# A fused attention and routed-layer kernel: the reads of block numbers gathered at first-layer tiles 2 to 5, one remainder placed inside a routing step, one quarter-sum moved into the next step

## The reference, cut to what matters

```
def _mlp(x, W1, b1, W2, b2):
    return gelu(x @ W1 + b1) @ W2 + b2           # exact gelu, 256 -> 256 -> 256

xn = layernorm(x)
q, k, v = _mlp(xn, ...q), _mlp(xn, ...k), _mlp(xn, ...v)
scores  = (q k^T) / sqrt(256 * 512) * tril       # linear attention, causal, no softmax
x1      = x + layernorm(scores @ v) * ln_w + ln_b
idx     = argmax over 8 tiles of position_table . sign(tile_sigs)     # by position only
out     = x1 + layernorm(x1) @ W[idx].T + b[idx]                      # one of 8 weights per row
```

## Time and profile before

| | us |
|---|---|
| median of 3 runs (lowest, highest) | 304.71 (304.62, 305.18) |
| the profiled execution: its own time | 304.78 |
| its span, first to last instruction | 303.0 |
| PE busy | 281.8 (93%) |
| VectorE busy | 237.2 (78%) |
| ScalarE busy | 191.6 (63%) |
| GpSimd busy | 168.1 (55%) |
| mean granted TensorE clock | 0.992 |

### The profile page before, as it was taken

How to read it: one execution, slowest core, us unless ns; L and a number is a source line. 1 busy time by engine, 2 the same in 40 slices (tenths; PEclk the granted TensorE clock), 3 DMA queues, 4 the chain that set the end, 5 groups by cost and what they waited for, 6 DMA issues and landing times.

```text
span 303.0 us, 5527 instructions
## 1 busy us (share of the span) xinstructions
PE 281.8 (93%) x1818; PEld 252.7 (83%) x1818; DVE 237.2 (78%) x549; ACT 191.6 (63%) x389; POOL 168.1 (55%) x230
## 2 busy tenths in 40 slices
PE   6869999999899999999999999999999898999970
PEld 6757988898789889888978898989898898999850
DVE  4587879889988978986898689678856879867660
ACT  2278568767666776678667866876877445787000
POOL 3902452172459184937554663648374476777771
PEclk9999999999999999999999999999999999999996
DMA  7816991002111211021121100017021460693220
GB/s 199 285 53 175 358 294 35 0 2 69 35 39 37 80 63 38 6 100 39 38 88 52 68 7 0 21 56 203 2 92 37 128 194 24 191 299 107 70 69 19
DMA packets 24193, 27.83 MB, mean 92 GB/s; under 512 B 4643, under 2 KB 22052, under 8 KB 24102
## 3 DMA queue, kind: packets, MB, share of 16 engines
q1 hardware_dynamic: 15750, 13.29, 15.0%
q0 software_dynamic: 3296, 8.64, 8.2%
q10 hardware_dynamic: 5120, 5.55, 5.8%
HBM read 13.95 MB, written 14.44 MB: 94 GB/s over the span
## 4 chain that ended last, share of the span: by engine, by line
PE 68%; DVE 13%; DMA 5%; POOL 4%; issue 4%; ACT 2%; SPq 1%; POOLq 0%; DVEq 0%; ACTq 0%
PE ring L475 40%; PE o_ps L475 10%; PE s_ps L475 6%; POOL out_dram L1697 3%; DMA w_stage<-w1v 3%; PE w_ps L475 2%; DMA slot_rows<-sorted_rows 2%; PE ring L488 2%; PE sc_ps L571 2%; DVE xres L1185 1%; DVE xnT L1113 1%; PE sc_ps L569 1%; DVE st L1192 1%; PE w_ps L614 1%; DVE w_sp L1329 1%
## 5 line engine op out<-in xcount | busy, mean ns | idle before, releaser
L475 PE MATMUL ring<-xnT,w_sp 128*128 128x512 f32 x288 | 73.4, 399 | 5.5 <-DVE hT L1118 3.5
L475 PEld LDWEIGHTS ring<-xnT,w_sp 128*128 128x128 f32 x288 | 51.9, 189 | 17.8 <-DVE hT L1118 4.8
L850 ACT ACTIVATE ring<-ring,b_cols 128x512 f32<-128x512 f32 x48 | 31.7, 660 | 24.8 <-PE ring L475 23.9
L475 PE MATMUL ring<-hT,w_sp 128*128 128x512 f32 x192 | 46.4, 396 | 0.0
L475 PEld LDWEIGHTS ring<-hT,w_sp 128*128 128x128 f32 x192 | 35.4, 188 | 8.1 <-DVE hT L1118 0.2
L1118 DVE TENSOR_TENSOR hT<-ring,hT 128x512 fp32r<-128x512 f32 x48 | 32.4, 680 | 12.3 <-ACT hT L853 12.0
L1650 POOL DMA_INDIRECT sorted_rows<-xres,slot_i x30 | 31.2, 1041 | 8.4 <-issue 6.6
L1616 POOL TENSOR_TENSOR vtok<-v,vtok 128x512 fp32r<-128x512 f32 x14 | 17.9, 1287 | 28.6 <-ACT vtok L870 28.6
L1597 POOL TENSOR_SCALAR nm<-mv 128x4 f32<-128x4 f32 x8 | 1.8, 231 | 52.2 <-DVE mv L1100 52.2
L853 ACT CAST hT<-ring 128x512 fp32r<-128x512 f32 x48 | 28.2, 587 | 1.5
L1697 POOL DMA_INDIRECT out_dram<-slot_rows x22 | 21.6, 981 | 6.7 <-issue 6.1
(11 more groups left out here) (238 smaller groups left out, 679.7 us busy)
## 6 DMA issues: line engine op xcount, KB each, us to landing
sorted_rows<-blank ACTq DMA_DIRECT2D x1, 5032.0 KB, 19.1
xt<-x SPq DMA_DIRECT2D x8, 512.0 KB, 3.6
slot_rows<-sorted_rows SPq DMA_DIRECT2D x22, 136.0 KB, 3.1
w_stage<-tile_w SPq DMA_DIRECT2D x8, 256.0 KB, 2.9
h<-sorted_rows SPq DMA_DIRECT2D x15, 136.0 KB, 3.1
hT<-position_table POOLq DMA_DIRECT2D x1, 512.0 KB, 8.1
sorted_rows<-xres,slot_i POOLq DMA_INDIRECT x30, 2.5
row_stage<-rows ACTq DMA_DIRECT2D x1, 384.0 KB, 8.1
```

Of the source, the lines that this page charges most:

```text
L475: last = te.matmul(o, lhs[k][a], rhs[k][c], start=start and k == 0 and i == 0, stop=stop and k == n - 1 and i == 2, skip_group_check=check)
L850: nc.scalar.activation(full, ring[(2 + m) % 3][:, :], ACT.Gelu, bias=b1c[:, m // 2, m % 2:m % 2 + 1]).then_inc(gelu, 1)
```

## The change: what it does

Three orders change; no instruction is added or removed.

1. In iterations 3 to 5 (`front_h` of steps 4, 5 and 6) each of the six tiles had two reads of block numbers ahead of it. Now tiles 0 and 1 have none, and tiles 2 to 5 have three each. The one read that is left for step 7 moves from tile 0 to tile 2.
2. The remainder of gelu tile 2, `h_rest(s + 1, 2)`, moves ahead of `lead_stat(s + 2)` in every iteration, and in iteration 1 ahead of both routing instructions; `route_chosen` now follows `lead_stat`, and its reduction, now `route_mine`, stands after `h_rest(s + 1, 3)`.
3. The last quarter of x1, `x1_final(s, (3,))`, stood ahead of `out_centred(s + 1, 0)`. It now stands in the next iteration, behind `h_rest(., 0)` and ahead of `x1_stats`.

```
             def front_h(s, ms, first):
                 for m in ms:
-                    if 4 <= s < 8:
-                        tile_number()
-                        tile_number()
+                    if 4 <= s < 8 and m >= 2:
+                        for _ in range(3):
+                            tile_number()
...
+            def route_mine():
+
                 link(nc.vector.tensor_reduce(mine[:, 0:2 * CLASSES, :], chosen[:, :, :, :], AX_X, ALU.add))
...
             for s in range(LAST - 1):
                 h_rest(s + 1, 0)
                 if s:
+                    x1_final(s - 1, (3,))
                     x1_stats(s - 1, range(CH))
...
                 if s == 0:
                     route_blocks()
-                elif s == 1:
+                h_rest(s + 1, 2)
+                lead_stat(s + 2)
+                if s == 1:
                     route_chosen()
-                lead_stat(s + 2)
-                h_rest(s + 1, 2)
                 lead_var(s + 2)
                 h_rest(s + 1, 3)
+                if s == 1:
+                    route_mine()
                 state_rest(s, 2)
...
                 state_rest(s + 1, 0)
-                x1_final(s, (3,))
                 out_centred(s + 1, 0)
...
             h_rest(LAST, 0)
+            x1_final(s - 1, (3,))
             x1_stats(s - 1, range(CH))
```

## The result

The changed kernel took 306.89 us in the median of 16 executions (305.6 to 308.8), the kernel before 304.95 in 16 beside it (304.53 to 306.35); the ratio is 1.0049, with a 95% interval of 1.0031 to 1.0067. It is slower, and its median lies outside the range of 303.8 to 306.1. Yet the profiled execution took 305.60 us with a span of 303.7, where 305.5 and 303.7 were forecast.

What follows compares the result with a forecast made beforehand. TensorE, 68% of the span, was taken to bound the kernel. Terms +0.54 + 0.37 - 0.20 = +0.71 us on the profiled 304.78 gave 305.5 us, range 303.8 to 306.1.

Steps and rivals of the forecast that it cites:

- Edit 1: Reads, iterations 3 to 5: tile 1's waits go (-1.76), later tiles wait (+1.77), slow first read +0.36; in sum +0.37 us.
- The losses at tiles 3 and 5: Iterations 3 to 5: behind the moved reads, tile 3 is late by 0.11 us and tile 5 by 0.48 each iteration.
- seventeen matmuls: TensorE's queue ahead of tiles 2 and 4: reads start with about seventeen matmuls still ahead, which limits how many are hidden.
- rival A: TensorE's sequencer runs further ahead, so the moved reads are hidden: -1.4 us, 303.4, faster; chance 0.13.
- Edit 2: Iteration 1: tile 5's wait goes, but the state's remainder ends at 81.22 and chunk 3 starts later: +0.54 us.
- TensorE's idle time ahead of tile 5 is moved behind it and grows: Iteration 1: the 1.08 us wait ahead of tile 5 moves ahead of chunk 3, which starts 0.54 us later.
- Edit 2 in the other iterations: Gelu tile 2's remainder and the statistics change places outside iteration 1: costed at nothing.
- The named cover: Outside iteration 1 TensorE waits for neither remainder nor statistics; without that, some 0.5 us an iteration.
- Edit 3: Moved quarter-sum: VectorE gains 0.5 to 1.5 us in six iterations; only iteration 6's first block transposes gain, -0.20 us.
- B: Iteration 1: chunk 3 doesn't become the next wait, as the state's remainder ends early enough: -1.0 us, 303.8; chance 0.06.
- C: Iteration 3: the first read's slow start isn't repeated or falls into spare time: +0.35 us, 305.1, no change; chance 0.28.
- the first read's 0.36 us: Iteration 3: the slow first read now heads six reads, so its 0.36 us come out in full at tile 3.

Runs made afterwards that it cites:

- best: The kernel before with the last quarter's sum moved and thirteen reads per iteration, only in the second layer of iterations 3 to 5: 307.49 us, 1.0077.
- best2: The kernel before with the last quarter's sum moved and reads in iterations 3 to 5 split over tiles 2 to 5 and the second layer: 302.72 us, 0.9931.
- only_remainder: The kernel before with only the move of gelu tile 2's remainder and its routing order: 306.89 us, 1.0037.
- only_sum: The kernel before with only the last quarter-sum of x1 moved to the next iteration: 304.49 us, 0.9976.

## Why the prediction was wrong

- **Edit 1** (+0.37): right, +0.44, which includes the -0.10 behind tile 5. The losses at tiles 3 and 5 came out within 0.13 us each, and reads never started with clearly more than seventeen matmuls ahead. So rival A, and with it the 64 entries that the Trainium skill gives (Advanced Engine Details and Errata, section Engine Queue Depths), don't show in this kernel; `best` and `best2` bear the count out from either side.
- **Edit 2** (+0.54): the delay was right to 0.02 us for the remainder's end, by the luck of two misses of 0.16 and 0.15 us that cancel. **The step that failed** is the last of that part, "TensorE's idle time ahead of tile 5 is moved behind it and grows", priced by its delay alone. It joins 1.08 us and what is added to one wait of 1.91 us, behind which the clock fell to 0.54 in an upper execution of `only_remainder`, for 1.5 us more. The sum had no term for that, nor for a group of slower executions at all, which the kernel before has too. It holds for the lower group, 305.6 to 306.1, and not for the median. A term of 1.3 us in about half of the executions would have put the median anywhere from 305.9 to 307.
- How often it happens was measured only by groups: 25 of 52 against 21 of 91. The changed kernel's median was 306.89, 305.89 and 306.57 in three sets, with 9 of 16, 4 of 12 and 6 of 12 in the upper group; with about half in each, chance decides on which side a median falls. That the median lies 0.8 us above the range and 1.4 above the forecast is owed in part to that, but 305.5 was below all three. The medians of the two other sets, 305.89 and 306.57, lie on either side of the range's end.
- **Edit 2 in the other iterations**, costed at nothing: 0.44 us at 140.20 in `only_remainder`. The named cover, that TensorE waits for neither there, was not enough by itself; in the changed kernel the lateness that edit 1 brings at tiles 3 and 5 hides it.
- **Edit 3** (-0.20): -0.25, and the quarter-sum takes 0.48 us nearly everywhere. `only_sum` is faster by itself, and gains 0.19 us more at tile 5 of iteration 1.
- **Rivals** B and C didn't occur in the profile: chunk 3 was the next wait, and some 0.3 of the first read's 0.36 us came out at tile 3 (0.43 in iteration 3 against 0.16 and 0.12). Of D there was a trace, the 0.09 us at tile 4 of iteration 4, which the prediction had left with nothing to spare.

What stays open: whether the wait at 20 us makes the whole upper group of the kernel before. Two executions of other kernels show the clock falling there; filling the wait didn't remove the group, by a cause that is only argued. How much of the changed kernel's upper group belongs to either place isn't shown. No upper execution of the changed kernel itself was profiled; that its clock falls just ahead of the second layer is taken from `only_remainder`, with the same wait at the same place.

## What to carry to other kernels

Two short waits of TensorE need not cost the same as one long one: where an edit joins or lengthens an idle stretch, look at the granted clock behind it in several executions, since one profile shows one of the groups. Work that moves from one place to another is paid for by the next instruction in the same queue that somebody waits for, so list those on the engines behind as well. And a long row of instructions that only the sequencer runs, like the thirteen reads of `best`, is hidden by what was queued before the whole row, not before each piece; an edit's lateness can also hide the cost of another, so the costs of parts that were timed alone need not add up.

## What the runs showed of the hardware

- TensorE's granted clock fell behind a wait of 1.91 us in one execution, to 0.54 of full speed from 82.9 to 86.3 us, and stayed at 1.00 behind the same wait in four others that were profiled. Behind the 2.4 to 2.6 us of the start-up it fell in two and stayed in eight. The Trainium skill (TensorE: Matmul & The Clock Gate, section Part 1: The HAM clock gate) has two levels for it on a chip where one core works, 1.2 and 2.4 GHz; the trace agrees, since the slow matmuls of 256 columns start 0.21 us apart (83.24 to 83.88 for three) in place of 0.12 (82.85 to 83.21 in the changed kernel).
- TensorE's reads of numbers take about 0.64 us each in a row (`best`: thirteen from 137.2 to 145.5), and matmuls that stand between them neither slow them down nor, in that row, refill the lead.
- No read started with clearly more than seventeen matmuls ahead of it. The one ahead of tile 2 in iteration 3 started at 127.3 us in the kernel before and in the changed one alike, though the latter has no reads ahead of tile 1.
